# Packing a half-empty chunk, splitting expert weights in two parts, and sharing the weighted sums between two engines

## The reference, cut to what matters

```python
def _swiglu(x, wg, wu, wd):
    return silu(x @ wg) * (x @ wu) @ wd

# mixture 0: 8 experts of 176 hidden columns, 2 picks a token, a shared expert of 704
probs = softmax(x @ Wr)
routing_weights, selected = top_k(probs, 2)
C = einsum('tk,tke->te', routing_weights, one_hot(selected, 8))
moe_out = einsum('te,eth->th', C, expert_out)
out = moe_out + sigmoid(x @ Wsg) * _swiglu(x, Sg, Su, Sd)

# mixture 1: 16 experts of 176 hidden columns, 4 picks a token, a shared expert of 352
scores = softmax(xt @ Wg.T)
topi = top_k(masked, 4)[1]               # of the two best of four groups of experts
combine = zeros((T, 16)).at[arange(T)[:, None], topi].add(take_along_axis(scores, topi))
h = silu(einsum('td,eid->eti', xt, W1)) * einsum('td,eid->eti', xt, W3)
y = einsum('etd,te->td', einsum('eti,edi->etd', h, W2), combine)
out = y + silu(xt @ Ws1.T) * (xt @ Ws3.T) @ Ws2.T
```

## Time and profile before

| | us |
|---|---|
| median of 3 runs | 785.82 |
| lowest, highest | 785.49, 788.51 |
| the profiled execution | 784.7 |
| its span, first to last instruction | 782.8 |

### The profile page before, as it was taken

One profiled execution on the slowest core, in us unless ns is written; L12 is line 12 of the kernel. 1 busy time (PEld: TensorE's weight loads), 2 busy tenths in 40 slices (PEclk: granted clock), 3 DMA queues, 4 the chain that ended last, 5 costly groups with the idle time before them and its releaser, 6 DMA issues. The chain is left out here.

```text
span 782.8 us, 12268 instructions
## 1 busy us (share of the span) xinstructions
PE 693.8 (89%) x3946; PEld 553.4 (71%) x3946; DVE 574.1 (73%) x1075; ACT 441.8 (56%) x969; POOL 394.0 (50%) x331
## 2 busy tenths in 40 slices
PE   7598877999999997899999999999979698899950
PEld 3144433598888887799998989888768566778740
DVE  6999999755353356898988888888878967544437
ACT  3887764353443334877777667666743267544430
POOL 0699878144675554454434332232313368777730
PEclk9799999999999999999999999999999999999985
DMA  4747521110353601111111006000039222333327
GB/s 144 285 163 250 179 68 40 62 41 23 100 143 116 215 28 35 55 62 41 62 61 35 15 22 246 2 2 1 21 116 380 86 71 85 89 101 103 101 88 235
DMA packets 38823, 77.66 MB, mean 99 GB/s; under 512 B 5345, under 2 KB 20394, under 8 KB 37738
## 3 DMA queue, kind: packets, MB, share of 16 engines
q1 hardware_dynamic: 34088, 64.41, 24.3%
q0 software_dynamic: 4512, 12.33, 5.2%
q10 hardware_dynamic: 162, 0.14, 0.1%
HBM read 59.07 MB, written 17.79 MB: 98 GB/s over the span
## 5 line engine op out<-in xcount | busy, mean ns | idle before, releaser
L1184 PE MATMUL psum<-xT_hi,w_ring 128*128 128x512 f32 x272 | 91.1, 395 | 1.0 <-ACTq L285 0.7
L2501 ACT ACTIVATE a_p_exp<-psum,a_nmax 128x256 f32<-128x256 f32 x128 | 59.6, 471 | 56.5 <-DVE a_nmax L2670 56.5
L2600 POOL TENSOR_TENSOR a_rr<-a_ss,eps 128x8 f32<-128x8 f32 x32 | 6.6, 207 | 156.8 <-DVE a_ss L2651 156.8
L641 POOL TENSOR_TENSOR m_dbu<-m_du,m_b_all 128x1024 f32<-128x1024 f32 x31 | 74.0, 2408 | 9.4 <-DVE m_du L727 6.9
L735 DVE TENSOR_TENSOR_SCAN m_hst<-psum,m_dbu 128x1024 f32<-128x1024 f32 x32 | 72.9, 2280 | 0.0
L1961 POOL DMA_INDIRECT expert_rows<-y_rows,f_puts_i x47 | 53.9, 1146 | 26.0 <-ACT y_rows L1907 15.0
L1320 POOL TENSOR_TENSOR f_h_lo<-f_hid,f_h_hi 128x512 fp32r<-128x512 f32 x34 | 44.0, 1295 | 44.4 <-ACT f_h_hi L1294 43.8
L387 PE MATMUL psum<-m_hc,ident 128*128 128x512 f32 x128 | 62.8, 614 | 0.0
L2364 PE MATMUL psum<-a_kT,a_qT 128*128 128x256 f32 x256 | 60.5, 379 | 1.4 <-ACT a_kT L2493 1.4
L1956 POOL DMA_INDIRECT x_rows<-norm_rows,f_rows_i x47 | 46.1, 982 | 28.8 <-DVE f_rows_i L2114 14.8
L1184 PEld LDWEIGHTS psum<-xT_hi,w_ring 128*128 128x128 f32 x272 | 51.1, 188 | 11.9 <-issue 1.5
(11 more groups left out here) (313 smaller groups left out, 2233.9 us busy)
## 6 DMA issues: line engine op xcount, KB each, us to landing
expert<-in_experts SPq DMA_DIRECT2D x16, 608.0 KB, 8.4
m_b_all<-b_rows SPq DMA_DIRECT2D x8, 1024.0 KB, 5.9
w_raw<-in_moe SPq DMA_DIRECT2D x20, 384.0 KB, 3.3
k_raw<-m_side SPq DMA_DIRECT2D x16, 256.0 KB, 2.0
a_keys<-k_raw SPq DMA_DIRECT2D x16, 256.0 KB, 2.6
norm_rows<-xn SPq DMA_DIRECT2D x8, 512.0 KB, 8.3
added<-expert_rows SPq DMA_DIRECT2D x16, 256.0 KB, 5.8
fold_in<-in_w_fold SPq DMA_DIRECT2D x8, 384.0 KB, 3.4
```

The lines of the kernel that those rows point to most:

```text
L641: pool.tensor_tensor(dbu[:, k % DBU_RING, :, :], du[:, h, :, :], b_all[:, n:n + 1, :].to_broadcast([P, G, HALF]), ALU.mult).then_inc(dbu_r ...
L1184: mm = pe.matmul(dst, a[part], b[of], start=(k == 0 and i == 0), stop=(k == KD - 1 and i == 2), skip_group_check=True)
L2501: ins = act.activation(pe_[:, n % 2, m, :], bank(hh)[:, tile * L:(tile + 1) * L], ACT.Exp, bias=nmax[:, n % 2, m:m + 1], accum_out=rsum[:, ...
```

## The change

Three parts of the kernel change, and nothing of mixer and attention.

**Mixture 0, the sixth shared chunk.** Of its 128 hidden columns 64 are in use. The host now puts the 64 columns of up behind the 64 of gate in the gate's weights (and the down rows twice), so that one product of 128x512 gives gate in partitions 0 to 63 and up in partitions 64 to 127 of one bank. Steps 7 and 11 make 6 products for `gate_up` and not 12; silu reads rows 0 to 63 and writes rows 64 to 127 of `f_sg`, and the DVE and ACT operations and the `down` products of these steps work on rows 64 to 127. The transfers and the making of the chunk's weight parts keep their size, and so does POOL's `f_h_lo`. Counts of the semaphore `up_ps` go by a table (`UPS`), since two steps no longer raise it.

**Mixture 1, the experts' parts.** An expert's 1216 columns are split in a part of 704 (gate and up) and one of 512 (down). Both parts of expert 15 are made before the blocks (on ACT ahead of the last `hidden_hi`, on DVE ahead of block 0's `b_hid`); then experts 12, 13, 14, 0 to 11 follow, two parts behind each of blocks 0 to 11 (three behind 5 and 8) and one behind each of blocks 12 to 15. `places` moves ahead of the wait for the last `down`, and `weights_found` from before block 0 to behind block 18.

**The end.** After `weights_picked` DVE makes 16 diagonal matrices `diag` (128x128, a pick's weights on the identity; picks 2 and 3 of 8 token tiles). For each quarter PE multiplies the diagonals with picks 2 and 3 (4 fp32 products of 128x256 into one bank); DVE adds picks 0 and 1 as before (4 operations) and then the bank (one operation of 128x512). SP's fetches keep their order; a store waits for 5 operations a quarter and not 8.

```diff
+PACKED = 704 // P
+PACKED_STEPS = 2
+PK = 704 % P
+SPLIT_AHEAD = 1
+WIDE_SPLITS = (5, 8)
+UPS = [sum(1 for c, h in STEPS[:j + 1] if c != PACKED) for j in range(len(STEPS))]
...
+                    if packed(j):
+                        for k in range(KD):
+                            f = slice(k * P, (k + 1) * P)
+                            mm = product3(pe, gate_bank(j), (w.gu_hi[c % RING][:, f], w.gu_lo[c % RING][:, f]),
+                                          (sh.xT_hi[:, k, tok], sh.xT_lo[:, k, tok]), k == 0, k == KD - 1)
+                        mm.then_inc(mix.gate_ps, 1)
+                        return
...
-                    act.activation(sg[:, j % HS, :], gate_bank(j), ACT.Silu).then_inc(mix.silu_s, 1)
+                    act.activation(sg[rows(j), j % HS, :], gate_bank(j)[0:PK if packed(j) else P, :], ACT.Silu).then_inc(mix.silu_s, 1)
...
+        early = list(range(experts - 1, experts - 1 - SPLIT_AHEAD, -1))
+        parts = [(e, part) for e in early + [e for e in range(FP32_BLOCKS, experts) if e not in early] + list(range(FP32_BLOCKS))
+                 for part in range(2)]
+        def halves_of(i):
+            if i < FP32_BLOCKS:
+                return 3 if i in WIDE_SPLITS else 2
+            return 1 if i < experts else 0
...
+                pe.wait_ge(diag_s, 2 * NT)
+                pe.wait_ge(y_s, NB)
+                for q in range(NT // 2):
+                    pe.wait_ge(added_in[q], 16 * picks)
+                    for t in (2 * q, 2 * q + 1):
+                        for k in range(2):
+                            mm = pe.matmul(bank(q)[:, (t % 2) * DM:(t % 2 + 1) * DM], diag[:, k, t, :], added[2 + k][:, t, :],
+                                           start=(k == 0), stop=(k == 1), skip_group_check=True)
+                    mm.then_inc(picked_ps, 1)
...
                 for j in range(J0 + 1, J1):
                     gated(j)
+                    if j == J1 - 1:
+                        act.wait_ge(w.up_ps, J1 - PACKED_STEPS)
+                        act.wait_ge(sparse.experts_in, 16 * experts)
+                        for n_ in splits_behind(-1):
+                            expert_high(n_)
                     hidden_hi(j)
...
-                    if i < experts:
-                        expert_low(i)
+                    for n_ in splits_behind(i):
+                        expert_low(n_)
+                    if i == FP32_BLOCKS + 6:
+                        weights_found()
                 weights_picked()
+                dve.wait_ge(y_ps, NB)
+                for t in range(NT):
+                    for k in range(2):
+                        dve.tensor_scalar(diag[:, k, t, :], ident[:, :], weights_of[:, 2 + k, t:t + 1], None, ALU.mult).then_inc(diag_s, 1)
...
-                    for k in range(picks):
+                    for k in range(2):
...
+                    dve.wait_ge(final, 5 * q + 4)
+                    dve.wait_ge(picked_ps, q + 1)
+                    xs = x[:, 2 * q:2 * q + 2, :].rearrange("p t f -> p (t f)")
+                    dve.tensor_tensor(xs, xs, bank(q), ALU.add).then_inc(final, 1)
```

More of the change, by code:

```diff
@@ L1653, in splits_before @@
         def splits_before(i):
[L1655 removed]
+            return max(n for n, (e, _) in enumerate(parts) if i >= experts or FP32_BLOCKS <= e <= i) + 1
         def puts_of(r):
@@ L2159, in _, with expert_low @@
                 dve.wait_ge(padded, 1)
-                places()
-                weights_found()
+                def expert_low(n):
+                    e, cols = split_cols(n)
+                    if e < FP32_BLOCKS:
+                        dve.wait_ge(y_ps, e + 1)
+                    dve.wait_ge(split_hi, n + 1)
+                    at = expert_at(e, cols.start, cols.stop - cols.start)
+                    dve.tensor_tensor(experts_lo[:, at], experts_w[e][:, cols], experts_hi[:, at], ALU.subtract).then_inc(split, 1)
+                for n_ in splits_behind(-1):
+                    expert_low(n_)
                 def hidden_kept(i):
```

77 lines of the change are left out of this document (43 added, 34 removed).

## The result

The changed kernel takes 780.28 us (median of 6 runs, 776.58 to 782.92) against 785.33 for the kernel before (6 runs, 782.18 to 788.51): a ratio of 0.9932, interval 0.9910 to 0.9953, which is -5.3 us (-7.1 to -3.7). Two later comparisons gave 0.9887 (0.9835 to 0.9939) and 0.9889 (0.9858 to 0.9919), some -8.8 us by their ratios (the medians lie 7.9 and 8.7 apart). The forecast was 778.4, or -7.4 us (0.9906). Its profiled execution has a span of 778.1 us (782.8 before).

A forecast was written before the change was run, and what follows sets the result against it. PE bounds mixture 0, a two-block ring of 6.20 us blocks 0 to 14, DVE's adds the end; -1.9 - 3.5 - 2.0 = -7.4 takes 784.7 to 777.3, as a median 778.4 us, range 775.0 to 782.5.

The forecast's parts named there:

- A: Mixture 0, packed sixth shared chunk: -1.9 us, from -2.76 gross and +0.84 of PE waiting; bounds -1.4 and -2.76.
- B: Mixture 1, split experts: -3.5 us, from -2.1, +0.7, +0.4 and -2.5; bounds -1.5 and -5.4.
- C: The end, sums shared with PE: -2.0 us, last add at 778.1 for 780.21, last quarter bound by its landing.
- the ring gains little: Rival for mixture 1's blocks: two instructions where one stood, split experts give only -1.5 us, time 780.4; chance 0.15.
- chain of waits: Mixture 0: transfer, ACT's conversion, POOL's `f_h_lo`, then PE; with 0.54 us of slack, PE would wait 0.84 us.
- one gap of about 0.8 us: Sign in mixture 0: PE's only gap, some 30 us behind the first packed step; none would mean -2.76 us.
- The ring: Blocks 0 to 14, high part, low part, `b_hidT` copy: arc 2.31 for 2.66, -2.1 us over twelve blocks, third parts +0.7.
- The start: Ahead of block 0's `b_hid`: two low parts added, `weights_found` gone, `places` filling DVE's idle 0.59: +0.4 us.
- Blocks 12 to 16: Scatter 12 to scatter 15 at POOL's pace, 7.95 us for 10.43, without PE's wait for the last low part: -2.5 us.
- POOL: Blocks 0 to 14: scatters still stall while DVE reads two SBUF tensors, about 0.35 us a block, scatters near 1.35.
- POOL is free: Rival in mixture 1's blocks: smaller low parts don't stall POOL's scatters, split experts give -5.4 us, time 776.5; chance 0.14.
- signs of being wrong: Scatter 15 not at least 3 us earlier, or stores at the end with DVE waiting for PE and not landings.

The follow-up runs named there:

- the kernel without the wait: Changed kernel with packed steps' `down` over 128 rows, step 12 of mixture 0 making h's parts before later weight parts, no third parts: 777.06 us, ratio 0.9901.
- part A alone: Kernel before with only the packed chunk of mixture 0, experts and sums as before: 787.13 us against 786.80, ratio 0.9996.
- the second profile: Profile of the changed kernel run again without edits: 778.41 us (4 runs), ratio 0.9887 to the kernel before.
- part C alone: Kernel before with only the end's sums shared with PE: 784.09 us, ratio 0.9954.

## Why the prediction was right, step by step

**The sum** was -7.4: A -1.9, B -3.5, C -2.0. By stages it is A -1.4 to -1.9, B -3.8 to -4.6, C -2.2, together about -7.4 to -8.7; measured totals are -5.3 and twice -8.8. The likeliest case came true. The first total alone (780.28) would fit the rival "the ring gains little" (780.4) as well; B's stages rule that one out. The mechanisms held in the main, but several terms were off and cancelled, and that is luck.

**Part A** is right in size, and its chain of waits is real. The gross price of 2.76 (2.68 in the kernel without the wait) was there, and with full `down` products so was PE's wait at the `down` of step 12: 0.95 for a forecast of 0.84, and 1.2 of the gross gain lost with the slower start behind it. In the changed kernel itself most of the loss is another: the `down` products on 64 rows, for which the prediction had no term, cost 0.84. It cancels almost, because PE would have waited anyway; part A alone has these 0.84 and no wait. That they equal the forecast wait is luck. In my list of signs "one gap of about 0.8 us" would have misled: the changed kernel shows it only as 64-row products and a remainder of about 0.2 to 0.5 at that `down`.

**Part B.** *The ring*: forecast -2.1 + 0.7 = -1.4 for scatters 0 to 12, measured -1.78. Timeline of the changed kernel's arc:

```profile
632.81 1.30 ACT L1937 ACTIVATE experts_hi<-expert 128x704 fp32r<-128x704 f32 x2
633.62 1.55 DVE L2227 TENSOR_TENSOR experts_lo<-expert,experts_hi 128x704 fp32r<-128x704 f32 x2 [0.58 <-ACT experts_hi L1937]
...
635.10 0.41 DVE L2237 COPY b_hidT<-psum 128x256 f32<-128x256 f32 x1
```

From the high part to the copy it is 635.10 − 632.81 = 2.29; the step said 2.31, against 2.66 in the earlier trace rows, and the ring of two blocks is 5.83 for a forecast of 5.85. But two terms were mis-sized and cancel: twelve blocks without third parts gain 1.36 and not 2.1, and the third parts gain 0.3 to 0.4 more where +0.7 was forecast as their cost. *The start*: forecast +0.4, measured -0.15 (37.35 to 37.20, both without a half-clock stretch). *Blocks 12 to 16*: forecast -2.5, measured -2.65, with the way from scatter 12 to 15 at 7.78 for 7.95; but 0.75 of the gain is the clock of the earlier trace rows, which parts A and C alone, with the same code, don't have. PE's wait there, 1.69 in the earlier trace rows, is now

```profile
672.28 0.42 PE L164 MATMUL psum<-experts_hi,b_xT_hi 128*128 x1 [0.20 <-DVE experts_lo L2227]
```

and the clock of that stretch is full:

```profile
670.00:676.00 6.00, 5.18 (x35) 4.42 (x34) 3.21 (x8) 3.25 (x11) 4.69 (x5) 1.00 0.37 105
```

*POOL*: scatters were forecast near 1.35, and are shorter (1.12 against 1.457 in the earlier trace rows); in their place some gathers are long. Summaries of the two lines in the changed kernel:

```profile
L2020 POOL DMA_INDIRECT expert_rows<-y_rows,f_puts_i x15: 988/1120/1515, 632.0 to 672.6; - x15
...
L2015 POOL DMA_INDIRECT x_rows<-norm_rows,f_rows_i x15: 966/972/1662, 633.6 to 673.9; - x15
```

Two gathers take 1.66 and 1.29 here; in the kernel without third parts six take 1.46 to 1.67, while all scatters but the first two take 0.99 to 1.00. So the stall has moved from one transfer to the other, which the prediction didn't have. That it comes with the low part as an operation of two SBUF inputs is now shown; whether it is the second input or another trait of that operation, the runs don't separate. That POOL would otherwise be free to gain 5.4 ("POOL is free") is refuted by the same runs: without any stall B gains 0.2 more. The Trainium skill ("SBUF — State Buffer", "Who interferes with whom") says that a DVE instruction with at most one SBUF input, outside its 2-port modes, doesn't contend with GpSimd, and that one with two does when GpSimd reads SBUF. The reduction (0.987) and the low part (1.457) agree with that; the page's inference that `tensor_tensor` doesn't hold up descriptors is against 15 indirect scatters of 15 here.

**Part C** came out at its size, but in this profile not by its path. Timeline of DVE and PE at the end of the changed kernel, and the clock of three stretches:

```profile
758.36 3.22 DVE L2271 TENSOR_SCALAR diag<-ident,f_weights_of 128x128 f32<-128x128 f32 x16
...
763.18 1.79 DVE L2278 SCALAR_TENSOR_TENSOR x<-added,f_weights_of,x 128x256 f32<-128x256 f32 x4 [1.59 <-DMA added<-expert_rows]
...
767.14 0.69 DVE L2283 TENSOR_TENSOR x<-x,psum 128x512 f32<-128x512 f32 x1 [2.17 <-PE psum L1907]
...
769.98 0.69 DVE L2283 TENSOR_TENSOR x<-x,psum 128x512 f32<-128x512 f32 x1 [0.44 <-PE psum L1907]
...
772.18 1.99 PE L1907 MATMUL psum<-added,diag 128*128 128x256 f32 x8 [0.58 <-DMA added<-expert_rows]
...
774.84 0.69 DVE L2283 TENSOR_TENSOR x<-x,psum 128x512 f32<-128x512 f32 x1
```

```profile
763.00:766.00 3.00, 2.71 (x7) 2.21 (x8) 1.76 (x4) 0.00 (x0) 0.00 (x0) 0.50 1.01 337
766.00:770.00 4.00, 4.00 (x13) 3.27 (x12) 2.38 (x6) 0.00 (x0) 0.00 (x0) 0.61 1.09 353
772.00:775.00 3.00, 1.99 (x8) 1.44 (x8) 2.90 (x7) 0.00 (x0) 0.00 (x0) 1.00 0.46 161
```

The diagonals take 3.22 (2.7 to 5.0 forecast), inside the wait for the first quarter. The last quarter's products begin behind its landing and take 1.99 (1.9) at full clock; the first quarters' ran at half, as forecast. What the sum didn't have is that DVE waits for these: 2.17 in the first quarter and 0.44 in the second. So DVE, and not the landing, bounds the last quarter here: it gets there only at 773.01, its adds end at 774.80, behind PE's products (774.17), and the last add ends 3.35 behind that landing and not 2.7. The landing itself comes 17.8 behind scatter 46 and not 18.3, and -2.0 remains; that is luck. In the second profile and in part C alone the path is the forecast one: DVE waits 0.30 and 0.32 for PE's last products, and the last add ends 2.79 behind the landing.

**What failed** is a step that the prediction didn't have: it took everything between mixture 0 and the blocks as moving as a whole. There the profiles of unchanged code differ by up to 4.5 us (296.27 to 300.75), which is half of the gain. The range took it in only because the other bounds were wide. Through it one of the prediction's own signs of being wrong came up: scatter 15 starts 2.4, 2.8 and 1.4 us earlier in the three profiles and not 3 (675.2, 674.8 and 676.2 for 677.6), though from the first `f_h_lo` of mixture 1 it comes 3.1 to 4.4 earlier. The other sign, stores with DVE waiting for PE, came up in the first two quarters.

## What to carry to other kernels

Cut both spans at events that both programs have, and look at the stages that the change does not touch first: here they moved by as much as half the gain, with TensorE's clock, and one part alone showed no gain in total though its stage did. A saving on the full engine is worth what the next chain leaves: it was found by price at one instruction, and gained by putting that instruction's inputs ahead of the waiting transfer. A stall that is always there need not cost anything: scatters 0 to 12 were 6.7 us longer by it in all, and without it they end 0.1 us earlier. And a total that comes out right can hold terms that cancel: read each term in its own stage.

## What the runs showed of the hardware that was not expected

An indirect transfer on POOL that starts while DVE works on a `tensor_tensor` with two SBUF inputs ends 0.86 to 0.88 us behind that instruction, in 15 scatters of 15 (median 1.457 us against 0.992; 0.987 with a one-input reduction of 1.42 us in its place). A scaled copy of one input (0.79 us) held up gathers that had begun about 0.5 us before it (1.37 to 1.43 against 0.97). A first product over 64 rows behind products over 128 kept the next one off for 0.22 us and not 0.12. Granted clock in the same code fell to 0.50 in one execution and not in the next, with up to 4.5 us in attention alone (296.27 to 300.75).
